# Weighted values of two key tiles issued in one piece in six attention stages of a decoder kernel

## What is computed

```python
def proj(x, W, b):
    return (x @ W.T + b).reshape(bs, -1, HEADS, D_K).transpose(0, 2, 1, 3)
qh, kh, vh = (proj(q, Wq, bq), proj(k, Wk, bk), proj(v, Wv, bv))
scores = jnp.einsum('bhqd,bhkd->bhqk', qh, kh) / jnp.sqrt(jnp.float32(D_K))
scores = jnp.where(mask[:, None] == 0, jnp.float32(-1000000000.0), scores)
attn = jax.nn.softmax(scores, axis=-1)
ctx = jnp.einsum('bhqk,bhkd->bhqd', attn, vh)
return ctx.transpose(0, 2, 1, 3).reshape(bs, -1, INPUT_DIM) @ Wo.T + bo
```

## Time and profile before

| | us |
|---|---|
| median of three runs | 3296.5 (3295.6 to 3300.51) |
| the profiled execution | 3305.88 |
| its span, first to last instruction | 3303.9 |
| L0a, start of the first to start of the last weighing | 73 to 300 |
| L0x | 355 to 479 |
| L1x | 1105 to 1245 |
| L2x | 2263 to 2370 |
| L3a | 2583 to 2809 |
| L3x | 2868 to 3004 |

### The profile page before, as it was taken

How to read it: one execution, slowest core, us unless ns; L and a number is a source line. 1 busy time by engine, 2 the same in 40 slices (tenths; PEclk the granted TensorE clock), 3 DMA queues, 4 the chain that set the end, 5 groups by cost and what they waited for, 6 DMA issues and landing times. The chain is left out here.

```text
span 3303.9 us, 44333 instructions
## 1 busy us (share of the span) xinstructions
PE 2749.2 (83%) x16417; PEld 1292.8 (39%) x16464; DVE 2048.6 (62%) x4084; ACT 1324.3 (40%) x2262; POOL 940.7 (28%) x1193
## 2 busy tenths in 40 slices
PE   4997869977775897998998999977863999698998
PEld 1332324422222453355563444443432232354555
DVE  5885771149998554566683655656576876563444
ACT  1664553255442452212212433425541567254221
POOL 2110200068786110333342544552044110200000
PEclk9998789988777898999999999997875999798999
DMA  5221300000001410121230000003001220320000
GB/s 130 38 40 40 61 15 20 0 0 0 0 0 58 80 22 2 27 66 27 60 83 19 1 1 1 1 1 60 18 0 18 46 40 16 101 39 1 0 1 13
DMA packets 45494, 95.05 MB, mean 29 GB/s; under 512 B 14168, under 2 KB 33420, under 8 KB 39520
## 3 DMA queue, kind: packets, MB, share of 16 engines
q1 hardware_dynamic: 45280, 92.22, 12.7%
HBM read 46.20 MB, written 1.38 MB: 14 GB/s over the span
## 5 line engine op out<-in xcount | busy, mean ns | idle before, releaser
L1748 POOL TENSOR_TENSOR mamba_dbu<-mamba_du,mamba_b 128x512 f32<-128x512 f32 x128 | 235.2, 1838 | 56.1 <-DVE stream L1774 21.2
L1533 PE MATMUL ps<-stream,weights 128*128 128x512 f32 x256 | 171.0, 782 | 76.4 <-DVE stream L1784 58.7
L1774 DVE TENSOR_TENSOR_SCAN stream<-mamba_da,mamba_dbu 128x512 f32<-128x512 f32 x128 | 213.7, 1670 | 23.1 <-issue 11.9
L542 DVE TENSOR_REDUCE L3a_negmax<-ps 128x1 f32<-128x512 f32 x256 | 162.5, 684 | 52.7 <-PE ps L302 34.3
L542 DVE TENSOR_REDUCE L0a_negmax<-ps 128x1 f32<-128x512 f32 x256 | 162.5, 684 | 50.1 <-PE ps L302 45.6
L2606 DVE TENSOR_REDUCE skv_negmax<-ps 128x2 f32<-128x1024 f32 (+3 forms) x128 | 101.2, 798 | 129.9 <-PE ps L2449 129.9
L405 ACT ACTIVATE L0a_probs<-ps 128x512 f32<-128x512 f32 x256 | 143.7, 599 | 76.2 <-PE ps L321 65.1
L405 ACT ACTIVATE L3a_probs<-ps 128x512 f32<-128x512 f32 x256 | 143.8, 600 | 74.2 <-PE ps L321 62.9
L2668 ACT ACTIVATE skv_probs<-ps 128x1024 f32<-128x1024 f32 (+3 forms) x128 | 90.1, 704 | 187.0 <-PE ps L2475 187.0
L164 POOL TENSOR_SCALAR vareps<-mv 128x4 f32<-128x4 f32 x24 | 9.8, 408 | 510.0 <-DVE mv L1279 509.9
L189 PE MATMUL ps<-stream,xT 128*64 128x512 f32 x512 | 128.6, 619 | 13.3 <-DVE moa_v L2231 7.2
(11 more groups left out here) (620 smaller groups left out, 6642.7 us busy)
## 6 DMA issues: line engine op xcount, KB each, us to landing
moa_masks<-picked SPq DMA_DIRECT2D x32, 512.0 KB, 6.6
stream<-stream SPq DMA_DIRECT2D x32, 192.0 KB
stream<-gate_up_down_in SPq DMA_DIRECT2D x1, 4352.0 KB, 13.1
stream<-value_output_in SPq DMA_DIRECT2D x1, 4096.0 KB, 12.2
moa_gateb<-gates SPq DMA_DIRECT2D x32, 128.0 KB
stream<-ffn_in SPq DMA_DIRECT2D x1, 2888.0 KB, 9.7
L0a_qs<-L0a_qs SPq DMA_DIRECT2D x16, 128.0 KB
L0x_qs<-L0x_qs SPq DMA_DIRECT2D x16, 128.0 KB
```

The source lines that it names most:

```text
L542: dve.tensor_reduce(negmax[:, hh // G % 4, a, hh % G:hh % G + 1], ps[:, i % S_RING, :], AX.X, ALU.max, negate=True).then_inc(s["maxed"], 1)
L1533: pe.matmul(ps[:, SUM_BANK + j, :], k.ident, hc[:, (J * i + j) % RING, :], start=n == 0, stop=n == N - 1).then_inc(s["summed"], 1)
L1748: pool.tensor_tensor(dbu[:, m % RING, :], du[:, b % 2, j, :], bsb[:, i % B_RING, :], ALU.mult).then_inc(s["dbu_ready"], 1)
L1774: dve.tensor_tensor_scan(out=hs[:, m % RING, :], data0=da[:, m % RING, :], data1=dbu[:, m % RING, :], initial=0.0, op0=ALU.mult, op1=ALU.a ...
```

## The change

TensorE issues nothing at odd J and at each even J the products of the two quads before, one directly behind the other. The order and the sums within the PSUM bank stay as they were. `probs` holds three quads in place of two, 8 KB more per partition. The same edit is made in both functions.

```diff
-PB = 2
+PB = 3
...
-                        if a == 2 and 1 <= J <= QUADS:
+                        if a == 2 and J % 2 == 0 and 2 <= J <= QUADS:
+                            weigh(J - 2)
                             weigh(J - 1)
```

## The result

| | before | after |
|---|---|---|
| median of the runs | 3298.7 us (3295.6 to 3302.2, five runs) | 3330.8 us (3327.5 to 3337.2, five runs) |
| ratio | 1 | 1.0097, 95% interval 1.0083 to 1.0111 |
| profiled execution, its span | 3303.9 us | 3328.1 us |
| mean granted clock of TensorE | 0.906 | 0.912 |

The change costs 32 us, 1.0%. The two profiled executions lie only 24.2 us apart in span, since that of before (3305.9 us) was longer than all five of its runs. Where the difference lies is read best from the length of each stage, from the first to the last instruction that touches its tiles.

A forecast was written before the change was run, and what follows sets the result against it. It took TensorE and VectorE to bound the unmasked stages in turn, and TensorE the masked ones. 24 + 9.5 + 0 = +33.5 us on the profiled 3305.9 gave 3339.4, or 3330 against the median; range 3300 to 3353.

The forecast's parts named there:

- TensorE, 0.2 per pair: All six attention stages: each joined pair of pieces spares TensorE 0.2 us of start-up, 26 us over 128 pairs at most.
- Clean pair, 6.60 again: Self-attention, two quads without further work: 6.60 us before and after, gain 0, VectorE running dry once for 1.8 us.
- Pair with a split, 8.01: Self-attention pairs where VectorE splits the maxima at an odd quad: 7.11 to 8.01 us, since no weighing hides the split's 0.84.
- Projections, +1.7 in eleven steps: Self-attention: each projection or output step on TensorE delays VectorE by 0.1 to 0.35 us, some eleven times, +1.7.
- Tail of a self-attention, -0.8: Last eight quads of a self-attention, with no scores left: TensorE gains 0.2 us per pair, -0.8.
- Self-attentions, +24: The two self-attentions: about +12 us per stage, +24 for both.
- Without a mask, +9 to 10: Two unmasked cross-attentions: +0.7 us where the split delays odd quads, about +4 per stage, first +1 to 2 more.
- With masks, 0: Two masked cross-attentions: TensorE binds and saves 3.2 us per stage, split and residual give it back; net -1 to +1.
- TensorE as the bound: Rival, whole kernel: TensorE sets the time throughout, so the 26 us come off, 3271 us; 7%.
- No joining: Rival: the second piece waits or loads weights anew, so nothing is saved, 3353 us; 10%.
- The cancelling case: Rival: splits are mostly covered while tails and masked stages keep their gain, -8 to +6, 3297 us; 9%.
- The clock rival: Rival, unmasked stages: more TensorE waiting sends more stretches to 1.2 GHz, some 12 us, 3342 us; 8%.

The follow-up runs named there:

- joined_early_split: Changed kernel with self-attention scores one quad further ahead, moving the split of the maxima to even quads beside the joined piece; 3310.5 us, ratio 1.0032.
- joined_self: Kernel before with the whole edit, third probability buffer included, in the self-attention function only; 3323.7 us, ratio 1.0068.
- joined_half_max: Changed kernel with self-attention's maxima taken over 256 of the 512 columns; 3278.0 us, ratio 0.9937 to the kernel before.
- joined_three_banks: Changed kernel with three banks for self-attention's first scores and two for the turned ones; 3331.5 us, ratio 1.0103 to the kernel before.
- buffer_only: Kernel before with the third probability buffer alone, weighings where they were; 3299.5 us, ratio 0.9997.
- joined_cross: Kernel before with the whole edit, third probability buffer included, in the cross-attention function only; 3305.3 us, ratio 1.0018.
- joined_masked: Kernel before with pieces joined only in the two masked cross-attentions, L1x and L3x; 3292.8 us, ratio 0.9983.
- single_early_split: Kernel before, single pieces, with self-attention scores one quad further ahead and the split of the maxima in an even quad; 3297.3 us, ratio 0.9999.
- single_half_max: Kernel before, single pieces, with self-attention's maxima taken over 256 of the 512 columns; 3260.5 us, ratio 0.9884.
- single_three_banks: Kernel before, single pieces, with three banks for self-attention's first scores and two for the turned ones; 3317.7 us, ratio 1.0057.

## Why the prediction was right

Forecast 3330.0, measured 3330.8. Over the profiled execution before it said +33.5; the means by stage say +32.2. The mechanism, a saving on TensorE that becomes a starvation of VectorE and a split that loses its cover, is what the runs show. That the number is off by less than 1 us is luck, as the last lines of this list say. By its own steps:

- **TensorE, 0.2 per pair.** Right. 0.23 is spared between the neighbours of the piece, 0.20 in the clean pair of the kernels with half maxima. The bound "0, the second starts like a fresh one" did not come true. The Trainium skill (TensorEngine Tiling (Array Packing), Key Properties) says that changing the tiling mode drains the engine and changing the tile does not. The trace agrees, with 0.23 us for the pair of changes that is spared. With nothing else in the way the spared 0.2 would have made the kernel 26 us faster; it became 32 slower, since what an engine is spared is one thing and what waits for it another.
- **Clean pair, 6.60 again.** Right: 6.55. VectorE runs dry once for 1.5 to 1.7 us (1.8 was given).
- **Pair with a split, 8.01.** Right: 7.97, and +0.86 in most of them; the two in L0a that work of a batch had made 7.42 long before also take 7.97, so they grew by 0.55 only. The step is shown by the early split, which takes back 19 to 21 of the 32 us, some 13 of them clear of the clock. "-0.3 each" for the three pairs with the residual: -0.2 to -0.5.
- **The values, +0.6:** measured +0.45. **Projections, +1.7 in eleven steps:** -0.14 to +0.3 each; right in size.
- **Tail of a self-attention, -0.8.** Wrong. Its last four pairs changed by +0.28, +0.22, +0.66 and -0.45, +0.7 in sum. "TensorE gains 0.2 per pair" doesn't hold there, because ScalarE now stands where VectorE stood: four exponentials in a row take it 2.1 us, it has three banks of turned scores, and it runs dry over a piece. Before and then after, at the same place, and TensorE behind it:

```profile
291.24 0.60 ACT L405 ACTIVATE L0a_probs<-ps 128x512 f32<-128x512 f32 x1 [0.33 <-PE ps L321]
```

```profile
305.06 0.60 ACT L406 ACTIVATE L0a_probs<-ps 128x512 f32<-128x512 f32 x1 [1.19 <-PE ps L321]
...
306.69 0.39 PE L321 MATMUL ps<-L0a_qs,stream 128*128 128x512 bf16 x1 [0.59 <-ACT L0a_probs L406]
```

  The prediction put ScalarE down as having room, which is true of its share and not of these quads. This reading of the tail is from the timeline; no run tests it.
- **Self-attentions, +24.** Measured +28.9. Of the 5 us that lack, 3 are the tails. The rest can be a stretch of lower clock behind the output projection, which the prediction had nowhere (below): the four joined stages in that mean had eight of them, the eight single ones seven. At 1.6 us each that is 3 to 4 us for the two stages, an estimate.
- **Without a mask, +9 to 10.** Measured +11.1 by the means. The worked pair was near in each of its times: scores at 2.50 (2.50), end at 6.88 (6.80), so +0.6 for the +0.7. "In half of the pairs a projection covers the split, +0" was wrong: such pairs in L2x take 7.67 in place of 7.25 and 8.14 in place of 7.28.
- **With masks, 0.** Wrong: -7.8 by the means, of which some 2 to 3 are the clock of L1x, and -5.8 in the kernel that changes nothing else. The saving was rightly called real, 3.2 per stage (2.7 in L3x). What failed is the step that gave it back, the split that "breaks through the slack by some 0.15 in each odd quad" and the residual by 0.3: pairs of L3x take 8.90 in place of 9.14, 9.00 in place of 9.15, and 9.64 in place of 9.60 where work of the batch falls, so most of the 0.2 stays.

The errors, +5 and +1.5 on the one side and -8 on the other, nearly cancel. That they do is luck, and it is why the forecast is closer than its terms.

**The rivals.** TensorE as the bound holds in the masked stages alone. No joining fell with the row of sixteen passes. The cancelling case did not happen; joined_early_split comes nearest to it, with 9.5 us left in the self-attentions. The clock rival was placed in the stages without a mask: their granted clock is 0.87 in L0x and 0.98 in L2x, 0.86 and 0.94 before, so it did not happen there.

## What to carry to other kernels

Before two pieces of work on one engine are joined to save its overhead, look at what the other engine does during each of them. The gap of a piece is cover for the other engine's odd jobs, and halving the number of gaps uncovers the jobs that stood beside the gaps that went. Make such a change stage by stage, where the row between the pieces shows TensorE waiting for nothing (here the masked stages), or move the odd jobs to the gaps that stay. Shown here are the self-attentions and the masked stages of one kernel.

## What the runs showed of the hardware

**A stretch at 1.2 GHz behind the output projection.** After, in L0a, behind the output projection of a batch, the busy table (columns as above):

```profile
143.00:146.90 3.90, 3.90 (x20) 2.69 (x21) 1.06 (x2) 1.02 (x3) 0.00 (x0) 1.00 0.51 111
146.90:150.30 3.40, 3.40 (x16) 0.77 (x18) 3.10 (x11) 1.69 (x3) 0.00 (x0) 0.50 0.00 0
150.30:154.00 3.70, 2.99 (x16) 0.54 (x8) 2.51 (x9) 2.30 (x5) 2.35 (x3) 1.00 0.01 2
```

The clock is granted at half for 3.4 us, although TensorE is counted busy without a break in it and in the 3.9 us before. The piece inside takes longer, here beside the same place one batch later:

```profile
148.14 2.98 PE L335 MATMUL ps<-L0a_probs,L0a_v 128*32 128x512 f32 x16
...
213.34 1.92 PE L335 MATMUL ps<-L0a_probs,L0a_v 128*32 128x512 f32 x16
```

The pair of quads takes 11.1 to 11.2 in place of 9.57, 1.6 us more. Each execution has six such places (three batches in two self-attentions). With joined pieces four had the dip after, four in joined_self (one of them 12 us behind the projection, all others 2.5 to 3.9), one in joined_early_split, three in joined_half_max and four in joined_three_banks, so 16 of 30. With single pieces it was one before, one in buffer_only, two in joined_cross, three in joined_masked, three in single_early_split, none in single_half_max and four in single_three_banks, so 14 of 42. It comes in both forms. The higher count in the profile after makes some 5 us of the difference between the two profiled executions; whether joining makes it likelier, and what sets it off, these counts can't settle.

**A row of maxima is shorter than its parts.** One maximum of 512 columns takes 0.69 from start to end, eight in a row 4.88 (both in the fence of the clean pair), which is 0.60 for each after the first. What bounds a stage is the 0.60, and the mean duration on the page (683 ns) would have made VectorE's part 14% too long.
